# The local slot of a perceiver kernel in a new order: three buffers of turned probabilities, rows copied on VectorE, squares and weight parts on GpSimd

## What is computed

```python
def attn_layer(x, Wqkv, qs, ksc, Wo):              # Wqkv 256 x 3072, Wo 1024 x 256, 16 heads of 64
    q, k, v = jnp.split(x @ Wqkv, 3, -1)
    q = l2norm(sh(q)) * qs;  k = l2norm(sh(k)) * ksc
    q = q * cos * scale + rotate_half(q) * sin * scale      # k the same with 1 / scale
    out = local_attention(q, k, sh(v))             # windows of 64 rows, each sees itself and the one before
    return out @ Wo

def ffn_layer(x, g, bln, W1, b1, W2, b2):          # W1 256 x 1364, W2 682 x 256
    xn = (x - mu) / jnp.sqrt(var + 1e-05) * g + bln
    a, gate = jnp.split(xn @ W1 + b1, 2, -1)
    return a * jax.nn.gelu(gate, approximate=False) @ W2 + b2
# the second half of the columns is shifted by one row before each of the two; both are added to x
```

## Time and profile before

| | us |
|---|---|
| median of 3 runs | 2147.58 (2144.16 to 2148.34) |
| the profiled execution, as timed | 2145.24 |
| its span, first to last instruction | 2143.4 |
| local layers, first `turn_qk` to the end | 781 to 2143 |
| 22 slots, from the second to the last | 835.38 to 2069.12 |

### The profile page before, as it was taken

The page is one execution under the profiler, slowest core; times in us unless marked ns, Lnnn a source line. Parts: engine busy times, 40 slices in busy tenths (PEclk is TensorE's granted clock), DMA queues, the critical chain, the costliest instruction groups (busy, mean ns, idle before and its releaser), DMA issues.

```text
span 2143.4 us, 51804 instructions
## 1 busy us (share of the span) xinstructions
PE 2040.7 (95%) x17400; PEld 1704.1 (80%) x17400; DVE 1723.7 (80%) x4874; ACT 1392.7 (65%) x4026; POOL 550.3 (26%) x317
## 2 busy tenths in 40 slices
PE   5999999999998998999999999999999999999988
PEld 4787887887886676888888888888888888888877
DVE  6786787787676498898889888898889888988883
ACT  3776567567564355676767676866777676767653
POOL 2111111111111334232323233232323242323220
PEclk9999999999999999999999999999999999999999
DMA  3000000000000410021102011201120111011010
GB/s 120 8 10 1 7 12 1 7 12 1 6 26 0 140 31 15 13 72 33 56 14 72 14 58 31 72 14 46 44 73 14 34 57 52 25 33 55 14 33 20
DMA packets 50017, 72.10 MB, mean 34 GB/s; under 512 B 9429, under 2 KB 36869, under 8 KB 49541
## 3 DMA queue, kind: packets, MB, share of 16 engines
q1 hardware_dynamic: 47429, 64.30, 9.9%
q10 hardware_dynamic: 2368, 4.98, 0.6%
HBM read 51.58 MB, written 2.10 MB: 25 GB/s over the span
## 4 chain that ended last, share of the span: by engine, by line
PE 47%; issue 7%; DVE 4%; DMA 3%; ACT 3%; POOL 2%; SPq 1%; DVEq 0%; ACTq 0%; POOLq 0%
PE ps_loc L1722 17%; PE ps_loc L1830 7%; PE ps_loc L1799 5%; PE ps_loc L1761 4%; PE ps_loc L1841 4%; PE ps_loc L1772 4%; DMA late<-y_all 3%; PE ps_loc L1741 3%; PE ps_loc L1788 3%; POOL rnorm L2655 2%; PE ps_loc L1342 1%; ACT xnT_high L2077 1%; ACT pT L2060 1%; ACT xnT_loc L2077 1%; DVE w_low L2259 0%
## 5 line engine op out<-in xcount | busy, mean ns | idle before, releaser
L2655 POOL TENSOR_TENSOR rnorm<-norm_floor,half_loc 128x32 f32<-128x32 f32 x48 | 300.5, 6261 | 582.7 <-DVE norm_floor L2270 385.2
L1722 PE MATMUL ps_loc<-w_high,xT 128*128 128x512 f32 x1152 | 379.3, 410 | 0.7 <-ACT qk L2032 0.6
L2053 ACT ACTIVATE prob_loc<-prob_loc,top_loc 128x128 f32<-128x128 f32 x768 | 299.2, 402 | 45.2 <-DVE top_loc L2334 43.2
L718 ACT ACTIVATE prob<-prob,new_top 128x256 f32<-128x256 f32 x512 | 252.2, 497 | 0.0
L1722 PEld LDWEIGHTS ps_loc<-w_high,xT 128*128 128x128 f32 x1152 | 203.9, 189 | 51.4 <-issue 9.3
L2334 DVE CUSTOM_DVE_ANT_0 prob_loc<-ps_loc,const,rnorm 128x128 f32<-128x128 f32 x768 | 218.8, 345 | 28.0 <-PE ps_loc L1761 25.8
L1722 PE MATMUL ps_loc<-w_low,xT 128*128 128x512 f32 x576 | 228.5, 397 | 0.0
L2045 ACT ACTIVATE qT_loc<-ps_loc 128x512 f32<-128x512 f32 x96 | 57.4, 598 | 238.1 <-PE ps_loc L1741 238.1
L923 DVE CUSTOM_DVE_ANT_0 prob<-ps_cross,bias 128x256 f32<-128x256 f32 x512 | 184.7, 420 | 20.7 <-PE ps_cross L494 11.1
L1799 PE MATMUL ps_loc<-wo,qT_loc 128*128 128x256 f32 x768 | 169.8, 379 | 1.3 <-ACT qT_loc L2067 1.3
L1179 POOL TENSOR_TENSOR o<-o,alpha 128x1024 f32<-128x1024 f32 x32 | 61.0, 1906 | 425.1 <-DVE o L962 333.4
(11 more groups left out here) (214 smaller groups left out, 4869.0 us busy)
## 6 DMA issues: line engine op xcount, KB each, us to landing
w_raw<-in_ffn_Wqkv_dram SPq DMA_DIRECT2D x24, 512.0 KB, 5.7
w_raw<-in_ffn_Wqkv_dram SPq DMA_DIRECT2D x24, 256.0 KB, 3.9
wo<-in_ffn_Wo_dram SPq DMA_DIRECT2D x24, 256.0 KB, 3.5
v_mid<-v_even SPq DMA_DIRECT2D x24, 256.0 KB, 3.4
v_mid<-v_odd SPq DMA_DIRECT2D x24, 256.0 KB, 3.7
w<-in_ffn_W_dram SPq DMA_DIRECT2D x12, 341.0 KB, 3.3
w<-in_ffn_W_dram SPq DMA_DIRECT2D x6, 640.0 KB, 4.6
ctx_raw<-in_ctx_dram SPq DMA_DIRECT2D x12, 256.0 KB, 2.8
```

The source lines that it names most:

```text
L718: ins = act.activation(prob[:, t, h, :], prob[:, t, h, :], ACT.Exp, bias=new_top[:, t, h:h + 1], scale=-1.0, accum_out=chunk_sum[:, t, h:h ...
L1722: ins = pe.matmul(ps[:, DENSE + j % 2, :], xT[:, px, kk, t * P:(t + 1) * P], wqkv[pw][:, kk, col:col + 512], start=kk == 0 and n == 0, sto ...
L2053: ins = act.activation(pr, pr, ACT.Exp, bias=top[:, h, t:t + 1], scale=-1.0, accum_out=total[:, h, t:t + 1])
L2655: pool.tensor_tensor(rnorm[:, b % 2, t, :], norm2_floor[:, :], half[:, :], ALU.pow).then_inc(rnorm_done, 8)
```

## The change

Buffers: pT has three buffers instead of two, so `probs_out` of pair p waits for the `out` of pair p-3's group. The normalised rows are turned into bank 4 and x into bank 5, both when minima 0 to 5 have read the scores, and no longer into the banks of `project` and `widen`. The second copy of the normalised rows (`xn_copy`) goes from ScalarE to VectorE. The squares of tile 0 go from ScalarE to GpSimd, between the b2 add and `rotate`. Of the twelve low parts, pieces 0 to 7 go to GpSimd (two after slot 2's `rotate`, six after the tables), and 8 to 11 stay on VectorE, in slot 3. ScalarE runs a one-column exponential after `q_out`, copies projection 0 ahead of `exps` 0, and has `exps` 7 ahead of `probs_out` 3. TensorE turns the normalised rows ahead of projection 11. VectorE's list is new throughout. The core of the diff:

```diff
-    pT = sb("pT", [P, 2, 2, TT, P])
+    pT = sb("pT", [P, TURNED, 2, TT, P])                      # TURNED = 3
+        XN_TURN, X_TURN, FIRST_X = 4, 5, DENSE + 1
 # TensorE, slot
                 turn_probs(a, 3)
+                if ffn:
+                    turn_xn(f, a)
                 if ahead:
                     project(n, nb, 11)
-                if ffn:
-                    turn_xn(f, ahead)
+                turn_probs(a, 4)
                 out(a, L, b, 1)
-                turn_probs(a, 4)
                 if turn:
-                    turn_x(L + U * (b + 2), (b + 2) % B)
+                    turn_x(L + U * (b + 2), (b + 2) % B, a)
                 turn_probs(a, 5)
 # ScalarE
             def probs_out(a, pair):
-                act.wait_ge(o_full, a + 4 * (pair // 2))
+                act.wait_ge(o_full, a + (4 * ((pair - TURNED) // 2 + 1) if pair >= TURNED else 0))
                 q_out(a)
+                act.activation(exp_warm[:, :], zero[:, :], ACT.Exp)
+                if ahead:
+                    qkv_out(n, nb, 0)
                 exps(a, 0)
-                if ahead:
-                    qkv_out(n, nb, 0)
...
-                exps(a, 7)
                 probs_out(a, 5)
                 if ffn:
                     gates(f, 0)
+                    gates(f, 1)
+                if ahead:
+                    squares(n, 1)
                 probs_out(a, 6)
 # VectorE, slot
                 minima(a, b, 1)
+                minima(a, b, 2)
+                inverse(a, 0)
+                share(a, 0)
                 if ffn:
                     moments(f, fb, shifts)
                 inverse(a, 1)
+                share(a, 1)
+                if ffn:
+                    normal(f, fb)
+                inverse(a, 2)
+                minima(a, b, 3)
+                if late:
+                    weights_low(L + LAYER, 8)
+                    weights_low(L + LAYER, 9)
+                minima(a, b, 4)
+                minima(a, b, 5)
+                share(a, 2)
+                if ahead:
+                    twists(n, nL, 0, 0)
+                inverse(a, 3)
+                share(a, 3)
+                if late:
+                    weights_low(L + LAYER, 10)
+                    weights_low(L + LAYER, 11)
+                minima(a, b, 6)
+                minima(a, b, 7)
+                inverse(a, 4)
+                share(a, 4)
+                if ahead:
+                    norms(n, 0)
+                inverse(a, 5)
+                share(a, 5)
+                if ahead:
+                    twists(n, nL, 0, 1)
+                inverse(a, 6)
+                share(a, 6)
+                if ffn:
+                    xn_copy(f, L if b else L - LAYER, fb)
+                    xn_low(f)
                 if ahead:
                     cosines_both(n, 0)
                 o_out(a, 1)
                 if ffn:
                     gated(f, 0)
+                inverse(a, 7)
                 share(a, 7)
                 if ffn:
                     gated(f, 1)
+                o_out(a, 2)
+                if ahead:
+                    sums(n, 0)
+                if ffn:
+                    gated(f, 2)
+                if ahead:
+                    norms(n, 1)
+                if turn:
+                    x_low(L + U * (b + 2))
+                if ffn:
+                    gated(f, 3)
                 if ahead:
                     twists(n, nL, 1, 0)
                     scaled_keys(n, (b + 1) % B, 0)
-                if ffn:
-                    gated(f, 2)
-                if split:
-                    weights_low(L + LAYER, 2)
-                if ffn:
-                    gated(f, 3)
                 if ahead:
                     twists(n, nL, 1, 1)
-                    norms(n, 1)
                     cosines(n, 1, 1)
# GpSimd
+            def squares(a):
+
+                pool.wait_ge(qkv_done, a + 4)
+                pool.wait_ge(norm2_done, a)
+                pool.tensor_tensor(square, qk[:, 0, :], qk[:, 0, :], ALU.mult).then_inc(square_done, 8)
                 for b in range(1, B - 1):
                     norm(L + U * (b - 1), i, b - 1)
+                    squares(L + U * (b + 1))
                     rotate(L + U * (b + 1), b + 1)
                 if not last:
+                    weights_low(L + LAYER, 0)
+                    weights_low(L + LAYER, 1)
                     pool.wait_ge(scale_in, loads(i * 32 + 64))
                     tables(L + LAYER, i + 1)
+                    for h in range(2, ON_POOL):
+                        weights_low(L + LAYER, h)
```

More of the change, by code:

```diff
@@ L1724, in project, with turn_qk @@
                 ins.then_inc(qkv_full, 1 if j < SLOTS - 1 else U - SLOTS + 1)
-            def turn_qk(a, first):
+            def turn_qk(a, first, turned):
                 pe.wait_ge(rope_done, a + U)
@@ L1731, in turn_qk @@
                     two, s = divmod(g, 2)
+                    if g == 1 and turned:
+                        pe.wait_ge(xT_done, a + 2 * U)
                     if g == 2:
@@ L1818, in widen @@
                         pe.wait_ge(w1_split_low, a + LAYER)
-                    pe.wait_ge(xnT_copied, a + U)
-                if m == 1 and turn:
-                    pe.wait_ge(xT_done, a + 4 * U)
+                    pe.wait_ge(xnT_high, a + U)
+                if m < 2:
+                    pe.wait_ge(u_done, a)
+                if m < 2 and ahead:
+                    pe.wait_ge(qkv_done, a + 2 * U + (SLOTS - 1 if m == 0 else U))
                 if m >= 2:
@@ L1874, in slot @@
                 n, nb = L + U * (b + 1), (b + 1) % B
-                turn_qk(a, b == 0 and not ffn)
+                turn_qk(a, b == 0 and not ffn, ahead)
                 scores(a, 0)
@@ L1916, in slot @@
                 if ffn:
[L1917 removed]
+                    widen(f, fb, 2, ahead)
                 turn_probs(a, 7)
                 if ffn:
[L1920 removed]
+                    widen(f, fb, 3, ahead)
                 out(a, L, b, 3)
                 if ffn:
[L1923 to L1924 removed]
+                    widen(f, fb, 4, ahead)
+                    widen(f, fb, 5, ahead)
                 project_out(a, b)
@@ L2117, in slot @@
                 if ahead:
-                    squares(n, 0)
                     qkv_out(n, nb, 4)
+                exps(a, 3)
                 probs_out(a, 1)
-                exps(a, 3)
                 if ahead:
                     qkv_out(n, nb, 5)
+                exps(a, 4)
+                if ahead:
                     qkv_out(n, nb, 6)
-                exps(a, 4)
                 exps(a, 5)
@@ L2128, in slot @@
                     qkv_out(n, nb, 7)
+                probs_out(a, 2)
+                if ahead:
                     qkv_out(n, nb, 8)
-                probs_out(a, 2)
                 exps(a, 6)
+                o_out(a, 0)
                 if ahead:
                     qkv_out(n, nb, 9)
-                o_out(a, 0)
+                exps(a, 7)
                 if ahead:
@@ L2146, in slot @@
                     x_out(L + U * (b + 2))
-                exps(a, 7)
                 probs_out(a, 5)
-                if split:
-                    weights_high(L + LAYER, 1)
                 if ffn:
                     gates(f, 0)
+                    gates(f, 1)
+                if ahead:
+                    squares(n, 1)
                 probs_out(a, 6)
                 if ffn:
-                    gates(f, 1)
+                    gates(f, 2)
+                probs_out(a, 7)
+                if ffn:
+                    gates(f, 3)
                 if split:
-                    weights_high(L + LAYER, 2)
-                    weights_high(L + LAYER, 3)
-                if ffn:
-                    gates(f, 2)
+                    for h in range(4):
+                        weights_high(L + LAYER, h)
+                o_out(a, 3)
                 if split:
                     weights_high(L + LAYER, 4)
-                probs_out(a, 7)
-                if split:
                     weights_high(L + LAYER, 5)
                 if ffn:
-                    gates(f, 3)
-                if ahead:
-                    squares(n, 1)
-                o_out(a, 3)
+                    gates(f, 4)
+                    gates(f, 5)
                 if split:
@@ L2395, in normal, with xn_copy @@
                 ins.then_inc(xn_done, U)
+            def xn_copy(a, L, b):
+                if b == 0:
+                    dve.wait_ge(vec_done, L + LAYER)
+                dve.wait_ge(xnT_done, a)
+                dve.wait_ge(xnT_high, a + U)
+                for kk in range(KD):
+                    ins = dve.tensor_scalar(xnT[:, kk, :], ps[:, XN_TURN, kk * T:(kk + 1) * T], vec[:, V_FG + kk:V_FG + kk + 1],
+                                            vec[:, V_FB + kk:V_FB + kk + 1], ALU.mult, ALU.add)
+                ins.then_inc(xnT_copied, U)
             def xn_low(a):
@@ L2425, in _, with slot @@
              first_y) = linear_vector(dve)
```

(10 more changed lines are left out.)

156 lines of the change are left out of this document (57 added, 99 removed).

## The result

The changed kernel takes 2191.68 us (median of 4 runs, 2190.67 to 2193.77), the kernel before 2146.93 in the same series: a ratio of 1.0216, 95% interval 1.0204 to 1.0229. It is slower, as forecast, but by 45 us and not by 20, and outside the range. The profiled execution has a span of 2189.8 us.

A forecast was written before the change was run, and what follows sets the result against it. Local slots were taken as bound by TensorE's work (floor 54.7 us). Slot losses made 22 slots 1258.0 against 1233.7: +24.3, -4 at the edges, +20.3 on 2145.24, 2165.5, plus half of 2.3: 2166 us, range 2128 to 2184.

The forecast's parts named there:

- the plain slot: A slot without weight pieces: 54.7 us floor plus losses of 0.25, 0.75, 0.9 and 0.2, giving 56.8 us.
- The stall before `turn_probs` 5: TensorE's 0.63 us wait for ScalarE to empty TURN, about 1.2 in slot 2, goes with three buffers.
- Squares hold `share` 2: GpSimd's squares, 4.6 us from +14.8, hold VectorE's `share` 2 to +20.0; the third `turn_probs` loses 0.75 us.
- Projection 3's 0.25: At the slot's start projection 3 waits for projection 1's later copy, starting at +10.9 instead of +10.68: 0.25 us lost.
- `widen` 5 waits for `gated` 3: VectorE's longer work before `gated` 3 ends it at +43.7, so `widen` 5 starts 0.9 us late (0.4 to 1.5).
- a side condition of 0.2 us: At the slot's end `gated` 5 ends at +51.5, so `narrow` starts 0.2 us later than +51.45.
- Slot 2, term 0.5 us: GpSimd's pieces 0 and 1 among `cosines` and `sums` can hold `gated` 4 and 5: 0.5 us (0 to 1.3).
- Slot 3, term 1.0 us: Pieces 8 and 9 delay the squares, `share` 2 ends at +21.3, pieces 10 and 11 add 1.2: 1.0 us (0.3 to 2).
- The third rival: In slot 3 squares slip between pieces 8 and 9; piece 9 and `minima` wait: +4 us five times, 2182 us; chance 0.10.
- only then can the squares start: In slot 3 GpSimd's squares begin only after VectorE's pieces 8 and 9 end, at +16.0.
- Edges: Last slot -2.5 us, first slot -1, the very end -0.5: 4 us taken off in all.
- rival 2: Faster: squares never hold VectorE, 2137 us, or 2125 with the `gated` chain ready in time too; together chance 0.30.

The follow-up runs named there:

- Number 5: The kernel before with only the third buffer of turned probabilities and the orders of `turn_probs` 4 and `probs_out` 4 it allows: 2151.42 us (ratio 1.0023).
- number 12: As number 10, but two buffers of turned probabilities, with `out` 1 ahead of `turn_probs` 4 on TensorE: 2175.94 us (1.0134).
- number 2: The changed kernel with the first tile's squares back on ScalarE, behind `probs_out` 0: 2175.87 us (1.0150).
- Number 4: The changed kernel with `gated` 3 ahead of `x_low` on VectorE: 2193.76 us (1.0237).
- number 7: The changed kernel with `gated` 3 ahead of `x_low`, and `gated` 4 and 5 ahead of the second tile's cosines and sums: 2159.51 us (1.0063).
- numbers 3: The changed kernel with GpSimd's weight pieces 0 and 1 behind the tables instead of ahead of them: 2180.28 us (1.0168).
- number 11: As number 10, but weight pieces 8 and 9 stay with VectorE between `minima` 3 and 4: 2138.97 us (0.9970).
- number 10: The changed kernel with `gated` as in number 7, squares on ScalarE, pieces 8 and 9 on GpSimd in the squares' place: 2135.85 us (0.9956).
- number 8: The changed kernel with all twelve weight pieces on GpSimd behind the tables, and `gated` as in number 7: 2165.06 us (1.0079).
- number 9: As number 8, but each weight piece on GpSimd waits for the piece before it to finish: 2170.85 us, a single run.
- number 6: The changed kernel with all twelve weight pieces' low parts on GpSimd and none on VectorE: 2174.37 us (1.0134).
- number 1: The changed kernel with VectorE's weight pieces 8 and 9 of slot 3 moved behind `share` 2: 2176.66 us (1.0154).

## Why the prediction was wrong

Its mean is made of parts that were right, three that were too small (slot 2, slot 3, the edges), and one that was too large (the plain slot).

**The stall before `turn_probs` 5.** Right that it goes. Number 5 adds that the old order got nothing from it, number 12 that the new one can't do without it.

**Squares hold `share` 2.** The mechanism was right, the duration not: 3.6 us and not 4.6, nearer the end of 3.8 that I took from twice 1.906. `share` 2 ended at +18.9 in place of +20.0, so `turn_probs` 2 lost nothing in a plain slot, where the term had 0.75. By number 2 the term is 0: VectorE would have spent the time waiting for ScalarE at `xn_copy`. Projection 3's 0.25 did not show either: it stood at +10.63.

**`widen` 5 waits for `gated` 3.** Forecast 0.9, measured 0.68 in most plain slots and 1.11 in others; `narrow` waited 0.18 for a forecast of 0.2. Yet as terms of a sum they were wrongly used. The slot was bound by VectorE: its length is the end of `gated` 5 (+50.56) and the 5.3 us of `narrow`. Number 4 removes the first wait and gains nothing. I had the end of `gated` 5 too, at +51.5, and wrote it down as a side condition of 0.2 us; it was the bound. My +51.5 was 0.9 us too late, as it carried the 1.0 us that `share` 2 and projection 3 were to lose. That gives the plain slot of 55.9 for the forecast 56.8, and 11 x 0.76 = 8.4 us that the sum had too much.

**Slot 2, term 0.5 us, measured 3.** I allowed one hold of at most 1.3 us. There were two, 0.87 and 1.05, on a chain of which I had said that it hardly has a gap, and then the clock: 1.7 us in three of five slots. The granted clock was 1.00 in the whole stretch before, and I took it for constant. 59.62 - 57.3 is 2.3 us, five times: 11.6 us.

**Slot 3, term 1.0 us.** The third rival came true, to which I had given 0.10. The step that failed is "only then can the squares start": I read from the earlier trace rows that back-to-back operations of VectorE keep GpSimd out, and the squares came in between two of them. In its place: piece 9 ends at +19.25 and not at +16.0, `share` 2 at +22.0 and not at +21.3, and `turn_probs` 2 waits 2.84 us. What lets GpSimd in at 1667.33 and kept it out at 1393.47 stays open. 61.19 - 57.8 is 3.4 us, five times: 17.0 us. With the 1.0 us that the term had, it measures 4.4; the rival's price, 4 us, was near. In three of the five the clock fell behind the stall, which is part of the 4.4.

**Edges.** I took 4 us off. From the last slot's start to the end it takes 74.6 us (before 74.3), still with a stall of 3.73 us before the first `turn_probs`; up to the second slot's start 0.3 more; and the second slot is 1.3 us longer, as `widen` 5 waits 1.14 us in it and `narrow` 0.18, where one wait of 0.63 stood before. (With `gated` moved, number 7, it takes 57.75 again.) That is 6.0 us too little. The last slot's part is uncertain by some 3 us: with the same lists in it, it took 74.7 us to the end in number 7 and 77.9 in numbers 3 and 4, with more time at the lower clock in the last two.

On the sum for the profiled execution: 2165.5 - 8.4 + 11.6 + 17.0 + 6.0 = 2191.7, beside 2191.6 measured. (With half of 2.3 added, 2165.5 gives 2166.7 and not the 2166 of the forecast, and rival 2's 2137 leaves that half out; neither changes anything.) That the mean came as near as 26 us owes something to luck, as the plain slots were forecast too long.

**What the change is worth without its accidents.** From 2191.7 moving `gated` 3 to 5 takes 32 us, squares back on ScalarE 20.5 (number 11), pieces 8 and 9 on GpSimd 3.1 (number 10): 2135.9, 0.44% below the kernel before. So the new order with its third buffer was sound in all but three places. My second rival gave 2137 us for the changed kernel; that number 10 lands there is chance, as its reason was another. That the first and last slots lose nothing or little to the change wasn't tried apart.

## What to carry to other kernels

Follow each engine's list to the end of the slot and take the latest of the arrivals; stalls found one by one along TensorE are not terms of a sum, as they are paid in the same time. Operations of VectorE that read SBUF, those with two inputs above all, and anything on GpSimd that reads SBUF are to be looked at in pairs, and what matters is what stands behind the held operation on its own engine: the same hold of 2 us cost 3 us per slot with `gated` behind it (59.6 against 56.6) and 0.2 without (55.8 against 55.6). When a buffer or an order is changed, ask of every other wait on the same buffer, not only of the one that stalls.

## What the runs showed of the hardware

- In three of five slots a row of GpSimd operations without a gap held one operation of VectorE through all that was left of it, 5.96 to 5.98 us for 0.69 us of work (number 8). In the other two it came in behind the piece under way (1.01 and 1.06 us), and so it did in all five where each piece waited for the one before, with gaps of 0.14 to 0.17 us (0.88 to 0.94 us, number 9). The Trainium skill ("SBUF — State Buffer", Who interferes with whom) says that VectorE and GpSimd share a pair of ports as an exclusive lock, that a VectorE instruction with two SBUF inputs contends for it with a GpSimd instruction that reads SBUF, and that issue order decides who blocks. The traces agree that they exclude each other; but in those three slots it wasn't one operation that VectorE waited for but the rest of the row. Where VectorE or GpSimd met the first operation of a row (pieces 0 and 1 in slot 2, the squares at piece 8) it did get in behind it. What makes the difference wasn't tried.
- In number 9 a VectorE operation of two columns with one input took 1.27 us beside the pieces; without them (number 6) it takes 0.17.
- After equal stalls of 2.0 to 2.8 us the granted clock fell to the lower level in some layers of one execution and not in others: behind the 2.04 us before `narrow` in three of five slots 2 of the changed kernel, in one of five in number 1, in four of five in number 6. Where it did, slot 2 was about 1.7 us longer.
- Squares of 128x2048 with one tensor as both inputs took 3.6 us on GpSimd, 1.9 on ScalarE (both in the changed kernel, the first and the second tile).
